# The transposes of the next group's rows, and ScalarE's copies of them, moved behind layer 0

## What is computed

```
xk = x0
for W, b in (w0, b0), (w1, b1), (w2, b2):
    z = relu(einsum('bhd,bkd,hks->bsd', x0, xk, W) + b)      # s = 128
    xk = z[:, :64]; direct.append(z[:, 64:])                  # the last layer: all of z
logit = sum over d of concat(direct)                          # 256 numbers per sample
h = relu([logit, dense_ctx] @ W_top1 + b_top1)
y = relu(h @ W_top2 + b_top2) @ W_top3
```

## Time and profile before

| | us |
|---|---|
| median of 3 runs | 2626.11 (2624.89 to 2628.14) |
| profiled execution, first to last instruction (span) | 2627.2 |
| TensorE busy | 2462.9 |
| VectorE busy | 2273.2 |
| GpSimd busy | 1559.0 |
| ScalarE busy | 1176.3 |
| moved by DMA | 477.02 MB, mean 182 GB/s |

### The profile page before, as it was taken

The page is one execution under the profiler, slowest core; times in us unless marked ns, Lnnn a source line. Parts: engine busy times, 40 slices in busy tenths (PEclk is TensorE's granted clock), DMA queues, the critical chain, the costliest instruction groups (busy, mean ns, idle before and its releaser), DMA issues.

```text
span 2627.2 us, 25816 instructions
## 1 busy us (share of the span) xinstructions
PE 2462.9 (94%) x7712; PEld 1439.5 (55%) x7712; DVE 2273.2 (87%) x1356; ACT 1176.3 (45%) x1414; POOL 1559.0 (59%) x1030
## 2 busy tenths in 40 slices
PE   0399999999999999999999999999999999999999
PEld 0155555555555555555555555555555555555553
DVE  0389989898998999899999989999898999989970
ACT  0144444444444444444444444444444444444442
POOL 6456666576666656665765666566566656732340
PEclk9899999999999999999999999999999999999999
DMA  2999999999999999999999999999999999999920
GB/s 61 182 200 201 200 185 197 193 193 186 200 198 188 194 192 199 189 194 196 191 196 186 202 190 194 193 194 195 184 200 185 198 194 197 194 187 196 194 47 0
DMA packets 262599, 477.02 MB, mean 182 GB/s; under 512 B 19371, under 2 KB 37675, under 8 KB 262501
## 3 DMA queue, kind: packets, MB, share of 16 engines
q1 hardware_dynamic: 242102, 471.34, 88.7%
q0 software_dynamic: 20480, 5.47, 1.7%
HBM read 468.99 MB, written 7.74 MB: 181 GB/s over the span
## 4 chain that ended last, share of the span: by engine, by line
PE 67%; POOL 10%; issue 7%; DMA 6%; DVE 6%; ACT 2%; SPq 1%; POOLq 0%; DVEq 0%; ACTq 0%
PE z L647 34%; PE z L670 29%; POOL emb L339 5%; DMA emb<-in_tbl,idx 5%; DVE prod L406 4%; POOL pair_lo L210 4%; PE xk L729 1%; DMA x_pairs<-x_transposed 1%; PE z L729 1%; ACT pair_hi L520 1%; PE turned L628 1%; POOL half_parts L206 1%; DVE logit L436 1%; DVE pair_lo L210 1%; ACT direct L581 0%
## 5 line engine op out<-in xcount | busy, mean ns | idle before, releaser
L406 DVE TENSOR_TENSOR prod<-x_pairs,xk 128x2048 f32<-128x2048 f32 x640 | 1439.5, 2282 | 142.3 <-PE z L670 107.0
L647 PE MATMUL z<-prod,w_plain 128*128 128x512 f32 (+2 forms) x2944 | 1401.5, 600 | 48.7 <-issue 27.0
L520 ACT CAST pair_hi<-prod 128x1024 fp32r<-128x1024 f32 x703 | 735.5, 1046 | 1122.3 <-PE z L670 780.6
L210 POOL TENSOR_TENSOR pair_lo<-prod,pair_hi 128x1024 fp32r<-128x1024 f32 x320 | 763.5, 2386 | 679.3 <-ACT pair_hi L520 663.9
L647 PEld LDWEIGHTS z<-prod,w_plain 128*128 128x128 f32 (+2 forms) x2944 | 561.6, 191 | 488.6 <-issue 407.7
L339 POOL DMA_INDIRECT emb<-in_tbl,idx x624 | 702.2, 1125 | 189.3 <-issue 176.6
L670 PE MATMUL z<-pair_hi,w_lo 128*128 128x512 f32 (+1 forms) x1408 | 793.2, 563 | 2.6 <-DVE pair_lo L210 1.7
L670 PE MATMUL z<-pair_lo,w_hi 128*128 128x512 f32 (+1 forms) x1408 | 556.8, 395 | 0.0
L670 PE MATMUL z<-pair_hi,w_hi 128*128 128x512 f32 (+1 forms) x1408 | 556.1, 395 | 0.0
L210 DVE TENSOR_TENSOR pair_lo<-prod,pair_hi 128x1024 fp32r<-128x1024 f32 (+1 forms) x384 | 468.1, 1219 | 49.5 <-ACT pair_hi L520 48.7
L670 PEld LDWEIGHTS z<-pair_hi,w_lo 128*128 128x128 f32 (+1 forms) x1408 | 267.0, 190 | 300.4 <-POOL pair_lo L210 139.9
(11 more groups left out here) (50 smaller groups left out, 567.0 us busy)
## 6 DMA issues: line engine op xcount, KB each, us to landing
x_pairs<-x_transposed SPq DMA_DIRECT2D x128, 2432.0 KB
x_diag<-x_transposed SPq DMA_DIRECT2D x192, 546.0 KB
x_pairs<-x_transposed SPq DMA_DIRECT2D x64, 256.0 KB
x_diag<-x_transposed SPq DMA_DIRECT2D x192, 78.0 KB
emb<-in_tbl,idx POOLq DMA_INDIRECT x624
x_transposed<-stage SPq DMA_DIRECT2D x32, 156.0 KB
x_transposed<-stage SPq DMA_DIRECT2D x32, 80.0 KB
x_pairs<-in_w SPq DMA_DIRECT2D x2, 704.0 KB, 7.0
```

Of the source, the lines that this page charges most:

```text
L210: engine.tensor_tensor(pair_lo[0:rows, pair % PAIR_RING], held[0:rows, at:at + 2, :], pair_hi[0:rows, pair % PAIR_RING].bitcast(F32), ALU. ...
L406: nc.vector.tensor_tensor(prod[0:rows, pos % RING, 0:n, :], a, xk.unsqueeze(1).broadcast_to([rows, n, N]), ALU.mult).then_inc(prod_ready, 1)
L520: nc.scalar.copy(pair_hi[0:rows, pair % PAIR_RING], held[:, at:at + 2, :]).then_inc(hi_ready, 1)
L647: ins = nc.tensor.matmul(z[n][:], w, held[0:rows, i, :], start=(k == 0 and i == plain[0]), stop=(k == last_slot and not here and i == plai ...
```

## The change

TensorE's call of `transpose_group` moves from before layer 0 to behind it, and ScalarE's call of `fill_stage` moves from behind the hand-over of layer 1 to behind `direct_0`. Nothing is added or taken out, and VectorE, GpSimd and SyncE keep their programs.

```diff
@@ ScalarE, group()
                     nc.scalar.activation(direct01[0:HALF], z[1][HALF:P], ACT.Relu, bias=b1_sb[HALF:P]
                                          ).then_inc(direct01_ready, 1)
-                    if c == 1 and not last:
-                        fill_stage(bt + 1)
                     if last and c == CHUNKS - 1:
                         round_splits(SPLITS[2], P, slot, pos, pair, held_by)
                     else:
...
                         hand_on(0, xk1, b0_sb, slot)
                         act.wait_ge(summed01, chunk + 1)
                         direct_0()
+                        if c == 1 and not last:
+                            fill_stage(bt + 1)
                         pair = round_splits(SPLITS[2][EARLY[2]:], P, slot, pos, pair, held_by)
@@ TensorE, group()
                     slot, pos = slot + SLX, pos + SLX
-                    if c == 1 and not last:
-                        transpose_group(bt + 1)
                     if not (last and c == CHUNKS - 1):
                         pair = layer(0, slot, pos, (chunk + 1) * len(SPLITS[0]), pair)
                         slot, pos = slot + SL0, pos + SL0
+                    if c == 1 and not last:
+                        transpose_group(bt + 1)
                     pe.wait_ge(summed2, chunk + 2)
```

## The result

The changed kernel takes **2719.44 us** (median of 4 runs, 2713.67 to 2723.25), the kernel before 2625.5 us (4 runs): a ratio of 1.0358, 95% interval 1.0335 to 1.038. It is slower, as forecast, but by 94 us where 41 were forecast, and outside the range (up to 2692). The profiled execution has a span of 2721.6 us and took 2723.25.

The account below looks back on a forecast made before the run. TensorE, VectorE and SyncE's DMA queue were all taken as close to full. Per group, -4.7 us for wait and clock and +7.4 for chunk 3's late loads gave +2.7, x 15 = 40.5 us: 2667 us, range 2622 to 2692.

Parts of the forecast that it names:

- TensorE's wait: Chunk 1 of each group: TensorE's 3.10 us idle until the gathers land goes, with the slow clock; at most 71 us gained.
- The copies come 9.6 us later: ScalarE's two copies to `stage`, now behind `direct_0` in chunk 1, end at 338.2 instead of 328.59.
- A: From the first product of chunk 1's layer 1 (300.5) to the first issue of chunk 3's `x_diag` (343.0).
- B: From the first issue of chunk 3's `x_diag` to the landing of its `x_pairs`: 39.5 us, bounds 38.6 and 43.6.
- `x_diag` is there after 12.6 to 15 us, ScalarE waits 4 to 7 us: Chunk 3's `x_diag`, issued at 343.0, lands at 355.6 to 358; ScalarE's copy waits, then TensorE idles 3 to 5 us.
- C: From chunk 3's first product of layer 1 to the next chunk 1's: two undisturbed chunks of 36.7 us, less 0.3.
- Rival A: Chunk 3's loads keep up and the whole gain of TensorE's move comes through: 2555 us; chance 0.15.
- Rival B: Chunk 3's two loads overlap on all DMA engines, landing 2.9 us earlier: taken as 2635 us; chance 0.15.
- Rival C: Chunk 3's `x_pairs` lands 4.1 us later, half of it counted, through gathers or slow clock: 2697 us; chance 0.15.
- the slow clock: TensorE's granted clock falls to 0.51 behind its idle time; layer 0's first slot takes 4.78 us, in chunk 0 3.11.
- Rival D: ScalarE's copies aren't later than now, because `direct_0` isn't what stands ahead of them; chance 0.02.

Follow-up runs that it names:

- the best version: The changed kernel with copies behind two roundings of layer 2 and SyncE's stores between chunk 3's `x_diag` and `x_pairs`, against the kernel before: 2560.8 us, ratio 0.9762.

## Why the prediction was wrong in size and right in kind

- *TensorE's wait goes.* Right. The transposes follow layer 0 without idle time. The gain of up to 71 us is real: the best version has 65 of it.
- *The copies come 9.6 us later.* Right: 14.6 us behind the end of layer 1, as worked out. From copies to `x_diag` it is 4.81 us, forecast 4.83.
- *A, from chunk 1's first product to `x_diag`'s issue.* Forecast 42.5 (343.0 - 300.5), measured 41.0. VectorE is late in chunk 1 too, and TensorE follows it at a shorter distance: in group 1 its layer 1 ends 21.4 us behind VectorE's first product (309.43 to 330.87), before 23.1 us (300.5 to 323.58). Worth -1.5 us a group.
- *B, "39.5 us in all; bounds 38.6 and 43.6".* **This term was mis-sized**: 42.1. I took the length from a trace in which `x_pairs` is issued 10 us behind `x_diag`, and argued that issuing it at 3 us changes nothing. It costs 1.8 us; holding it back to 8 us gives 1.4 of them back. The other 0.8 us is my guess of the old length, which is 40.3 by the semaphore and not 39.5. Worth +2.6 us.
- *`x_diag` is there after 12.6 to 15 us, ScalarE waits 4 to 7 us.* Again too short: 17.3 us, and a wait of 8.48 us in group 1. TensorE's longest wait is 6.8 us, where 3 to 5 were forecast.
- *C, the two chunks behind it.* **The second mis-sized term.** The sum used 155.1 - 82.0 = 73.1 us for the step from chunk 3 to the next chunk 1, so two chunks of 36.7 less a little that TensorE makes up. Measured 75.6: nothing makes the lateness good, and VectorE waits for `x_pairs` at nearly every chunk (51 times in the run). The landings of the next two `x_pairs` come 38.2 and 37.4 us apart (means of groups 1 to 13), before 36.8 and 36.9. That a late start would slow them I had put at nothing. Worth +2.5 us. Why they are slower isn't shown. It is not that the DMA engines can't do a chunk in less: in the best version the same landings are 36.1 and 36.6 us apart.
- Together -1.5 + 2.6 + 2.5 = +3.6 us a group, x 15 = 54 us: 2667 + 54 = 2721, against 2719. The error in A had the other sign and hid 22 us of the other two, by luck.

Rival A fell with SyncE's order as it is, and came true with the order changed. Rival B is refuted with a number: overlap on all engines gave no gain but a loss. Rival C had the right sign and place (late `x_diag` and `x_pairs`): the landing came 2.6 us later than I took it, of C's 4.1. But C let half of that count, and the group is A + B + C, so all of it did. The gathers, which it named, have at most a small part in it; the slow clock, which it named too, was not tried by itself. Rival D is excluded by the timeline.

Open: why the two chunks behind a late chunk 3 take 75.6 us and not 73.4, whether by the nearness of the two loads or by the pace of the DMA engines from a late start. Holding `x_pairs` back in all chunks by three products was too much to tell.

## What to carry to other kernels

An engine that moves a hand-over behind other work also moves every DMA that stands behind that hand-over in the issuing queue; read that queue's order before the engine's own. Where two moves go in opposite directions, run each alone: here one was worth -28 us, the other +130. And when DMA is near full, size a load by traces in which its neighbours stand at the same distance, and add what the following chunks no longer make good.

## What the runs showed of the hardware

Two loads issued close together kept more DMA engines busy and moved hardly more. While `x_diag` is loaded alone the share is 0.85 and the rate 169 GB/s; where `x_pairs` waits for it, with gathers beside it, 0.81 and 152 GB/s (351.5 to 364.5 of that run). With `x_pairs` issued 3 us behind it the share is 1.01 and the rate 162 GB/s (351 to 368 above), and `x_diag` itself takes 2.3 to 2.5 us longer. An estimate from these rows, with 2 KB = 2048 bytes and 16 engines: each 2 KB keeps an engine busy for 0.16 to 0.17 us in `x_diag` alone (0.85 x 16 x 2048 / 169000) and for 0.17 us in `x_pairs` alone (1.07 and 205 GB/s), but for 0.20 us while both are under way. The share of busy time alone would have shown a gain.

The prediction leaned on a rule from the Trainium skill (DMA: Bandwidth & Descriptors, "Why a DMA increments its semaphore by 16 and not by 1" and "Queues, rings and completion order"), by which 13 engines take part in `x_diag` and the early start of `x_pairs` gains nothing. The ratio of the shares, 0.85 to 1.07 or 0.79, is near 13 of 16, and nothing was gained. Measured, the early start costs 1.8 us, and the measurement decides. What the two loads contend for no run here shows.
